# Attention phase of a decoder block: sums transposed to rows of queries and divided there by VectorE, in place of selecting matmuls and spread reciprocals

## What is computed

```python
q = einsum('oc,bct->bot', Wq, target) + bq;  k, v = ... Wk, Wv of source   # heads of 16 channels
dot = einsum('bhdt,bhds->bhts', q, k) / 4
mask = target_mask[:, :, :, None] * source_mask[:, :, None, :]
dot = mask * dot - (1.0 - mask) * 1e6
amap = softmax(dot, axis=-1) * mask
out = einsum('bhts,bhds->bhdt', amap, v).reshape(b, 256, 512)
x = layernorm(x + out)
```

## Time and profile before

| | us |
|---|---|
| median of 3 runs | 3875.85 (3870.3 to 3878.94) |
| the profiled execution | 3874.5, its span 3872.7 |

### The profile page before, as it was taken

How to read it: one execution, slowest core, us unless ns; L and a number is a source line. 1 busy time by engine, 2 the same in 40 slices (tenths; PEclk the granted TensorE clock), 3 DMA queues, 4 the chain that set the end, 5 groups by cost and what they waited for, 6 DMA issues and landing times. The chain is left out here.

```text
span 3872.7 us, 54857 instructions
## 1 busy us (share of the span) xinstructions
PE 3297.6 (85%) x16801; PEld 1994.3 (51%) x16834; DVE 2991.5 (77%) x2878; ACT 2570.2 (66%) x4936; POOL 2219.4 (57%) x1448
## 2 busy tenths in 40 slices
PE   6878888888888888888866599889998999969998
PEld 4666566655665566655653244444444444324444
DVE  1999998989989899899996576666666666518887
ACT  3877777777878787777763166555555555637776
POOL 1888887878888788888884234333343344220000
PEclk8989999999999999999977699989998999979999
DMA  3011101121012101110111543444344433221111
GB/s 147 7 52 69 69 25 45 69 69 50 20 69 69 70 16 53 70 69 26 44 63 42 157 153 123 138 143 143 123 141 136 148 126 127 78 97 42 43 43 36
DMA packets 158019, 310.84 MB, mean 80 GB/s; under 512 B 22385, under 2 KB 77937, under 8 KB 157633
## 3 DMA queue, kind: packets, MB, share of 16 engines
q1 hardware_dynamic: 153424, 299.60, 23.4%
q10 hardware_dynamic: 4352, 8.39, 0.7%
HBM read 216.24 MB, written 91.69 MB: 80 GB/s over the span
## 5 line engine op out<-in xcount | busy, mean ns | idle before, releaser
L681 DVE TENSOR_TENSOR_SCAN states<-states,bu 128x1024 f32<-128x1024 f32 x512 | 1173.5, 2292 | 186.0 <-POOL bu L612 102.4
L612 POOL TENSOR_TENSOR bu<-du,bc 128x1024 f32<-128x1024 f32 x512 | 1195.7, 2359 | 113.4 <-DVE states L681 110.1
L545 ACT ACTIVATE states<-dt,negA 128x256 f32<-128x256 f32 x2048 | 850.4, 461 | 435.6 <-DVE hc L693 374.8
L1336 DVE TENSOR_REDUCE mmax<-s_ps 128x2 f32<-128x1024 f32 x512 | 624.6, 1224 | 412.7 <-PE s_ps L1051 401.5
L1167 ACT ACTIVATE pt<-s_ps 128x512 f32<-128x512 f32 x1024 | 582.8, 596 | 451.5 <-PE s_ps L1060 440.8
L421 PE MATMUL y_ps<-id_sb,hc 128*128 128x128 f32 x4096 | 577.6, 287 | 136.6 <-DVE hc L693 136.3
L693 DVE TENSOR_TENSOR hc<-states,bc 128x1024 f32<-128x1024 f32 x512 | 626.8, 1224 | 52.4 <-DVE states L681 0.9
L421 PEld LDWEIGHTS y_ps<-id_sb,hc 128*128 128x128 f32 x4096 | 494.2, 148 | 300.6 <-DVE hc L693 254.1
L1060 PE MATMUL s_ps<-qst,kst 105*128 105x512 bf16 x1024 | 397.3, 398 | 12.4 <-ACT pt L1167 5.4
L1051 PE MATMUL s_ps<-kst,qst 102*128 102x512 bf16 x1024 | 331.6, 408 | 63.9 <-DMA kst<-mask_d 57.1
L1069 PE MATMUL pv_ps<-pt,vaug 128*32 128x512 f32 x2048 | 288.8, 638 | 27.4 <-ACT o_sb L1192 26.8
(11 more groups left out here) (157 smaller groups left out, 4707.1 us busy)
## 6 DMA issues: line engine op xcount, KB each, us to landing
bc<-bc_scratch SPq DMA_DIRECT2D x128, 512.0 KB, 4.8
stack_d<-parts SPq DMA_DIRECT2D x192, 256.0 KB, 2.6
w_raw<-in_w_ffn SPq DMA_DIRECT2D x32, 768.0 KB, 5.6
qst<-stack_d SPq DMA_DIRECT2D x64, 384.0 KB
kst<-stack_d SPq DMA_DIRECT2D x64, 384.0 KB
x<-xres SPq DMA_DIRECT2D x32, 512.0 KB, 2.8
xT_sb<-in_xT SPq DMA_DIRECT2D x16, 512.0 KB, 3.6
xres<-in_x SPq DMA_DIRECT2D x16, 512.0 KB, 3.8
```

Of the source, the lines that this page charges most:

```text
L545: a = act.activation(states[:, bank, first:first + SEQ], dt[:, t, :], ACT.Exp, scale=negA[:, t, c * NS + n:c * NS + n + 1])
L612: pool.tensor_tensor(bu[:, buf, :].rearrange("p (n l) -> p n l", n=NS), du[:, t % (2 * GRP):t % (2 * GRP) + 1, :].to_broadcast([P, NS, SEQ ...
L681: m = dve.tensor_tensor_scan(dst, dst, bu[:, BU_OF[k][0], half * 2 * SEQ:(half + n) * 2 * SEQ], 0.0, ALU.mult, ALU.add)
L1336: dve.tensor_reduce(mmax[:, u // HG, c:c + 2], s1_ps[:, pair], AX.X, ALU.max).then_inc(s1_free, 1)
```

## The change

The three kinds den, rbc and num go, with the arrays `sel_den` and `sel_num`, the tiles `rdenx`, `rbc` and `ntmp` and the semaphores that went with them. In their place:

- turn (u = 4 to 7, one for each 128 queries): four fp32 transposes of 128x128 put the four groups' sums by query; DVE takes 16 reciprocals out of `misc` and with one scalar_tensor_tensor multiplies the numerators by the mask and by them, into `on_sb`.
- back (u = 9 and 13, one for each 128 channels): four transposes turn `on_sb` back by channel; DVE adds them to `xres`.
- The maxima come in three m steps instead of four (`MAXIMA`): groups 0 and 1 together at u = 10, group 2 at u = 14, group 3 at u = 0 of the next body. v moves from u = 10 and 11 to 11 and 12.
- ACT's copy of group 0 waits for the turns of the batch before, and no longer the copies of groups 0 and 2 for num. ACT loads ctx at u = 14 instead of 12.
- SP issues `max_rows` 0 ahead of q's parts, the store of x2 behind `load_group` 2, and the load of `nm` ahead of `load_group` 3.

```diff
-MISC = ((0, "m", 3, 0), (1, "k", 0, 2), (2, "k", 1, 2), (3, "q", 0, 2), (4, "den", 0, -1),
-        (5, "rbc", 0, -1), (6, "num", 0, -1), (7, "rbc", 1, -1), (8, "q", 1, 2), (9, "num", 1, -1),
-        (10, "v", 0, 1), (11, "v", 1, 1), (12, "m", 0, 1), (13, "m", 1, 1), (14, "m", 2, 1))
-
+MISC = ((0, "m", 2, 0), (1, "k", 0, 2), (2, "k", 1, 2), (3, "q", 0, 2), (4, "turn", 0, -1),
+        (5, "turn", 1, -1), (6, "turn", 2, -1), (7, "turn", 3, -1), (8, "q", 1, 2), (9, "back", 0, -1),
+        (10, "m", 0, 1), (11, "v", 0, 1), (12, "v", 1, 1), (13, "back", 1, -1), (14, "m", 1, 1))
+
+MAXIMA = ((0, 1), (2,), (3,))
 SPLIT_AT = {"k": 4, "q": 10}
-PER_BATCH = {"k": 2, "q": 2, "m": HGROUPS, "den": 1, "rbc": 2, "num": 2, "v": 2}
...
+        on_sb = sb("on_sb", [P, TT, HEADS, HDIM])
...
+        m_r = sb("m_r", [HG * TT, 2, P])
         m_parts = sb("m_parts", [HG * TT, HGROUPS, 3, P], BF16)
...
                 if not (isinstance(b, int) and b == 0):
-                    wait(m_in[g], b * 16)
-                wait(m_split, seq("m", b, g))
-                sp.dma_start(m_d[g].rearrange("a c t -> c a t"), m_parts[:, g]).then_inc(m_out, 16)
-                wait(m_out, seq("m", b, g) * 16)
-                sp.dma_start(qst[ROWS1:ROWS2, par, g * HG:(g + 1) * HG, :].rearrange("p h t -> p (h t)"),
-                             m_d[g].rearrange("a c t -> a (c t)")).then_inc(m_in[g], 16)
+                    for g in groups:
+                        wait(m_in[g], b * 16)
+                wait(m_split, seq("m", b, idx))
+                sp.dma_start(m_d[lo:hi].rearrange("g a c t -> c g a t"), m_parts[:, lo:hi]).then_inc(m_out, 16)
+                wait(m_out, b * (len(MAXIMA) * 16) + (idx + 1) * 16)
+                for g in groups:
+                    sp.dma_start(qst[ROWS1:ROWS2, par, g * HG:(g + 1) * HG, :].rearrange("p h t -> p (h t)"),
+                                 m_d[g].rearrange("a c t -> a (c t)")).then_inc(m_in[g], 16)
...
                     sp.dma_start(xres[:, :, :], rows(x1n_d, n, SEQ * HID).rearrange("(i p h) -> p i h", p=P, h=HID)).then_inc(xres_in, 16)
-                    sp.dma_start(nm[:, :], maskT_of(n)).then_inc(nm_in, 16)
                 if active(s):
                     if active(b):
                         wait(ev["v"], s * 2)
...
-                if active(n):
-                    wait(x2_ready, n * 2 + 2)
-                    sp.dma_start(rows(x2, n, SEQ * HID).rearrange("(i p h) -> p i h", p=P, h=HID), xres[:, :, :]).then_inc(x2_out, 16)
+                if active(s):
+                    max_rows(s, 1 - par, 0)
                 if active(f):
                     wait(q_split, f + 1)
                     store_parts(0)
...
-                if active(s):
-                    max_rows(s, 1 - par, 0)
                 if active(f):
                     wait(parts_out, (f + 1) * (12 * 16))
                 group(0)
                 group(1)
                 group(2)
+                if active(n):
+                    wait(ev["back"], n * 2 + 2)
+                    sp.dma_start(rows(x2, n, SEQ * HID).rearrange("(i p h) -> p i h", p=P, h=HID), xres[:, :, :]).then_inc(x2_out, 16)
                 if active(s):
                     max_rows(s, 1 - par, 1)
-                    max_rows(s, 1 - par, 2)
+                if active(b):
+                    if active(n):
+                        wait(ev["turn"], b * TT)
+                    sp.dma_start(nm[:, :], maskT_of(b)).then_inc(nm_in, 16)
                 group(3)
 
             run(sp, body)
...
-                elif kind == "den":
+                elif kind == "turn":
                     if part == 0:
                         pe.wait_ge(o_copied, (batch + 1) * HGROUPS)
-                    for tt in range(TT):
-                        for g in range(HGROUPS):
-                            product(misc[:, tt * HEADS + g * HG:tt * HEADS + (g + 1) * HG],
-                                    o_sb[:, g, tt * P:(tt + 1) * P], den_sb[:, :])
-                elif kind == "rbc":
+                    for g in range(HGROUPS):
+                        product(misc[:, g * P:(g + 1) * P], o_sb[:, g, idx * P:(idx + 1) * P], id2[:, :])
+                elif kind == "back":
                     if part == 0:
-                        pe.wait_ge(rdenx_ready, batch + 1)
+                        pe.wait_ge(ev["turn"], (batch + 1) * TT)
                     for tt in range(TT):
                         product(misc[:, tt * P:(tt + 1) * P],
-                                rdenx[:, tt, idx * 8:(idx + 1) * 8, :].rearrange("p h d -> p (h d)"), id2[:, :])
-                elif kind == "num":
-                    for a in range(2):
-                        for i in range(2):
-                            cols = slice(a * (HID // 2), (a + 1) * (HID // 2))
-                            product(misc[:, cols], num_sb[:, i, :], o_sb[:, 2 * idx + i, cols], i == 0, i == 1)
+                                on_sb[:, tt, idx * 8:(idx + 1) * 8, :].rearrange("p h d -> p (h d)"), id2[:, :])
                 elif part == 0:
 
-                    pe.wait_ge(s1_free, batch * 32 + (idx + 1) * HG * 2)
-                    pe.transpose(misc[0:HG * TT, 0:P], mmax[:, idx, :], id2[:, :]).then_inc(mm["m"], 1)
+                    pe.wait_ge(s1_free, batch * 32 + (MAXIMA[idx][-1] + 1) * HG * 2)
...
-                    m = pe.matmul(dst, lhsT, rhs, start=start, stop=stop)
+                    if kind in ("turn", "back"):
+                        m = pe.transpose(dst, lhsT, rhs)
+                    else:
+                        m = pe.matmul(dst, lhsT, rhs, start=start, stop=stop)
                 if products and part == 2:
                     m.then_inc(mm[kind], 1)
 
...
-                if g % 2 == 0 and not (isinstance(b, int) and b == 0):
-                    act.wait_ge(mm["num"], b * 2 - 1 + g // 2)
+                if g == 0 and not (isinstance(b, int) and b == 0):
+                    act.wait_ge(mm["turn"], b * TT)
                 act.activation(o_sb[:, g, :], pv_ps[:, :], ACT.Copy).then_inc(o_copied, 1)
 
...
                     for unit, kind, idx, off in MISC:
-                        if unit == u - 1 and kind == "rbc" and active(b + off):
-                            act.wait_ge(mm["rbc"], seq("rbc", b + off, idx))
-                            if not (isinstance(b, int) and b + off == 0 and idx == 0):
-                                act.wait_ge(ev["num"], seq("num", b + off, idx) - 1)
-                            act.activation(rbc[:, :], misc[:, :], ACT.Copy).then_inc(ev["rbc"], 1)
                         if unit == u - 1 and kind == "m" and active(b + off):
                             act.wait_ge(mm["m"], seq("m", b + off, idx))
                             if not (isinstance(b, int) and b + off == 0 and idx == 0):
                                 act.wait_ge(m_split, seq("m", b + off, idx) - 1)
-                            if not (isinstance(b, int) and b + off == 0):
-                                act.wait_ge(m_in[idx], (b + off) * 16)
-                            act.activation(m_parts[:, idx, 0, :], misc[0:HG * TT, 0:P], ACT.Copy)
-                            act.activation(m_r[:, :], misc[0:HG * TT, 0:P], ACT.Copy).then_inc(ev["m"], 1)
+                            count, g0 = len(MAXIMA[idx]), MAXIMA[idx][0]
+                            for g in MAXIMA[idx]:
+                                if not (isinstance(b, int) and b + off == 0):
+                                    act.wait_ge(m_in[g], (b + off) * 16)
+                            turned = misc[0:HG * TT, 0:count * P].rearrange("c (g t) -> c g t", g=count)
+                            act.activation(m_parts[:, g0:g0 + count, 0, :], turned, ACT.Copy)
+                            act.activation(m_r[:, 0:count, :], turned, ACT.Copy).then_inc(ev["m"], 1)
                     if active(b):
                         exponentials(b, u, 1)
-                    if u == 12 and active(f + 1):
+                    if u == 14 and active(f + 1):
                         if active(b + 1):
...
             pool.memset(kst.ap().rearrange("p a h t -> p (a h t)").bitcast(F32), MINUS_ONES).then_inc(preset, 1)
             pool.memset(half_neg[:, :], -0.5)
...
+                n, g0 = len(MAXIMA[idx]), MAXIMA[idx][0]
+                r, groups = m_r[:, 0:n, :], slice(g0, g0 + n)
+                pool.tensor_tensor(r, r, m_parts[:, groups, 0, :], ALU.subtract)
                 pool.drain()
-                pool.tensor_copy(m_parts[:, idx, 1, :], m_r[:, :])
+                pool.tensor_copy(m_parts[:, groups, 1, :], r)
                 pool.drain()
-                pool.tensor_tensor(m_parts[:, idx, 2, :], m_r[:, :], m_parts[:, idx, 1, :], ALU.subtract).then_inc(m_split, 1)
-
-            def spread_den(batch):
-
...
-                pool.wait_ge(ev["den"], batch + 1)
-                pool.tensor_tensor(rdenx[:, :, :, :], rden[:, :, :].unsqueeze(3).to_broadcast([P, TT, HEADS, HDIM]),
```

(40 more changed lines are left out.)

48 lines of the change are left out of this document (13 added, 35 removed).

## The result

The changed kernel takes 3782.36 us (median of 4, 3779.80 to 3785.51), the kernel before beside it 3874.51: ratio 0.9762 [0.9746, 0.9779], 92 us less. Its profiled execution took 3785.5 us with a span of 3783.6, against 3874.5 and 3872.7 before. The forecast was 3785. The total is met; two of the terms behind it are wrong by some 65 and 55 us (4.3 and 3.6 us in each of 15 batches), with opposite signs. That is what this part is about.

A forecast was written before the change was run, and what follows sets the result against it. PE's list of work was taken to bound the attention. Full batches 56, kst boundaries 18 and 2, the batch without successor 4 and the end 11 sum to 91 us less: 3785 us, range 3736 to 3848.

The forecast's parts named there:

- The instructions: Turn on DVE: reciprocal 0.3 us, product 0.48; back's addition on DVE 0.68; each transpose on PE 0.12.
- The new units: Attention, per batch: four turns of 3.9, 3.6, 3.6 and 3.8 us, backs 3.6 and 3.5, together 22.0 us.
- the 0.15 for hand-overs: Added to a turn unit's 3.45 us, since PE must wait for DVE to read the single misc buffer: 3.6.
- The wait at u = 8: ACT's copy of group 0 now waits for the last turn, delaying exponentials and PE's values: 0.2 to 0.6 us.
- The floor of 3.32: Under every short attention unit: 3.32 us, as in an m step, where PE waits for ACT's exponentials of s2_ps.
- The replaced units: Den, two rbc, two num and one m step of the kernel before take 26.0 us per batch.
- kst and the boundaries: PE's 2.0 us wait for the next batch's stacked keys goes: 18 us at 9 boundaries, 2 ahead of the first.
- not won: At about five boundaries the 2.0 us is lost again, PE waiting 2 us longer for the o_sb copy.
- vaug stays: PE's 1.74 us wait for DVE's vaug remains: vaug, at 6.7 us, still meets POOL's subtraction, about 5.5 to 7.6.
- rival B: Vaug comes after the subtraction and meets POOL's 4.09 us instruction; PE waits 4.2 us longer, 3848 us; chance 0.14.
- The end: Serial chain from the last o_sb copy to the store falls from 23.2 us to 12.3, 10.9 less.
- rival E: PE runs at half clock through the six short units: 288 us more, 4073 us, slower than before; chance 0.04.

The follow-up runs named there:

- e4: Changed kernel with plain fp32 matmuls against the identity in place of the 24 transposes a batch: 3815.59 us, ratio 0.9856.
- e7: Changed kernel with each turn's reciprocal done twice on DVE: 3801.96 us, ratio 0.9806.
- e1: Changed kernel with POOL's last step of the weights moved from u = 12 to the end of u = 9: 3732.29 us, ratio 0.9639.
- e12: Kernel before the change, with only POOL's last step of the weights moved to the end of u = 9: 3869.16 us, ratio 0.9994.

## Why the prediction was right, and where it was not

- **The instructions.** The DVE terms stand (0.248, 0.484 and 0.677 us for 0.3, 0.48 and 0.68). For the transposes e4 is the measure: 2.83 + 0.9 with two matmul instructions each came out as 3.73.
- **The new units.** 20.7 us for 22.0. What failed is the 0.15 for hand-overs and what I added at u = 4 for ACT's cast and copy: PE runs a turn's transposes while DVE is at a row maximum, so the hand-over is in time, and ACT has room. The wait at u = 8 is 0.53, in the 0.2 to 0.6.
- **The floor of 3.32.** For the m units value and reason were right: PE waits for ACT's exponentials there, in every batch. For the turn and back units the value was right and the reason wrong: PE's own list (3.27) and in the turns DVE's (3.24, an estimate) come to nearly the same length (e4, e7), and PE loses less than 0.05 us to the exponentials there. That all of these come out within 0.1 us of each other was luck.
- **The replaced units.** This step failed most: 26.0 us for 29.0. I read one batch, with the clock at 1.00 through den, and put the second rbc's length for the first. Of the 3.0, 1.9 are the lower clock beside den's small matmuls, 1.15 the first rbc's unit.
- **kst and the boundaries.** Away from a branch the pair of units fell from 8.4 to 6.8, 1.6 of the 2.0. At a branch it grew from 15.3 to 17.0; "not won" was wrong by 1.7, as the branch itself is longer than what it used to overlap.
- **vaug stays.** It failed, and rival B's mechanism is what happened: vaug met the weights' step (e1 shows it by 50 us, e12 that before it did not). I had vaug at 6.7 us and the subtraction until 7.6; counted from the scores just ahead of the unit's mark (2634.27) the trace has vaug at 7.0 and the subtraction until 7.0, so each link was off by less than 0.7, and the margin of 0.9 was gone. PE's wait grew by 3.82 - 1.74 = 2.1 us, not by B's 4.2, since it takes the place of the old wait and isn't added to it; with the lower clock behind it the two units grew by 3.6. I had B at 0.14 on a margin that a chain of ten links can't carry.
- **The end.** 11.2 us for 12.3, against 23.2 in the earlier trace rows. Timeline of the changed kernel, last copy and last store:

```profile
3347.50 0.60 ACT L1187 ACTIVATE o_sb<-pv_ps 128x512 f32<-128x512 f32 x1 [3.84 <-PE pv_ps L1066]
...
3358.68 0.40 SPq L1022 DMA_DIRECT2D x<-xres  x1
```

- **The clock (rival E).** In the turn units it was full; the window has 96 matmul records and a granted clock of 1.00:

```profile
2613.00:2630.00 17.00, 16.47 (x96) 6.85 (x96) 14.08 (x18) 11.07 (x20) 10.63 (x5) 1.00 0.33 113
```

The rule of the Trainium skill that I had set against the change ("TensorE: Matmul & The Clock Gate", Part 4, on the PE-mode transpose: transposes don't count as activity the way matmuls do) shows no effect in this mix of transposes and matmuls; whether it holds for transposes alone, no run here shows. If anything the old code had the trouble: it was den's matmuls of four columns beside which the clock fell.

So the total was right by luck: 3.0 + 1.3 us per batch of gain that I had not seen met 3.6 + 0.8 of loss that I had not seen. With B's mechanism and my sizes for the rest I would have said 3848. The sum by units, not the total, says what was understood.

## What to carry to other kernels

Cost a removed step from all its batches, not from one: list the marks of a unit through the whole stage before you take a length, and look at the granted clock beside each. When two engines write close to each other, ask what the other has queued next, since a pair of instructions that starts 0.1 us too late can wait out the whole next one; moving that one (4.17 us of POOL, for which PE does not wait) gave 50 us, more than half of what the change itself did. A wait put down to a copy or "issue" once per pass of a loop may be the branch: write the loop out once and see.

## What the runs showed of the hardware

- Two DVE instructions of 128x256 took 0.62 us alone, 2.49 beside a POOL instruction of 2.12, and 4.45 when they started 0.05 us after one had ended and the next, of 4.17, began 0.13 us after them.
- After a wait of 3.8 us of PE the next four fp32 matmuls of 128x256 took 1.91 us, against 1.03, at a granted clock of 0.83 over those 10 us; a wait of 1.74 was followed by 1.90 in one batch and by 1.03 in the next.
- PE, busy without a gap and with 32 instructions of four columns among the rest, went below a granted clock of 1.00 in 12 batches of 13; with 128x128 transposes between other matmuls it stayed at 1.00 in all.
- The branch back of the loop cost 6.9 us each time in the one kernel and 10.2 in the other, in a stage that PE paces.
- A reciprocal of 128x16 from the accumulation buffer took 0.248 us and one of 128x64 0.557: as an estimate by the two, 0.145 us whatever the width and 6.4 ns for each column.
